# Two layers of cross-attention in fp32: scores in two rounded products instead of three, with the halves of the queries brought together by DMA

## The reference

```
q = x @ Wq;  k = ctx @ Wk;  v = ctx @ Wv          # fp32
s = softmax(q_h @ k_h.T / sqrt(16))               # per head, 256 x 77
x = x + concat_h(s @ v_h) @ Wo + bias
```

## Time and profile before

| | |
|---|---|
| median of 3 runs | 932.49 us (929.38 to 933.43) |
| span of the profiled execution | 926.1 us; its own time is not given beside it |
| TensorE matmul busy | 903.4 us (98%) |
| TensorE weight load busy | 681.3 us (74%) |
| VectorE busy | 685.7 us (74%) |
| ScalarE busy | 544.6 us (59%) |
| GpSimd busy | 402.8 us (43%) |
| granted TensorE clock, mean | 0.997 |
| DMA | 112.41 MB, 80526 packets, queue of SP busy 44.4% of 16 engines |

### The profile page before, as it was taken

How to read it: one execution, slowest core, us unless ns; L and a number is a source line. 1 busy time by engine, 2 the same in 40 slices (tenths; PEclk the granted TensorE clock), 3 DMA queues, 4 the chain that set the end, 5 groups by cost and what they waited for, 6 DMA issues and landing times.

```text
span 926.1 us, 28090 instructions
## 1 busy us (share of the span) xinstructions
PE 903.4 (98%) x11518; PEld 681.3 (74%) x11518; DVE 685.7 (74%) x1221; ACT 544.6 (59%) x549; POOL 402.8 (43%) x229
## 2 busy tenths in 40 slices
PE   8899999999999999999999999999999999999897
PEld 5777778777787777777777777777778777777665
DVE  3775787868778686787868688786786868678557
ACT  4456565656556556666556656556665656656553
POOL 3424263633436263366624446364344625433224
PEclk9999999999999999999999999999999999999999
DMA  6313534445444544545555444544534544443342
GB/s 203 102 32 80 138 93 132 135 124 148 98 119 119 164 131 110 149 115 140 141 148 140 102 118 113 137 132 123 134 95 118 139 131 134 102 130 78 86 134 94
DMA packets 80526, 112.41 MB, mean 121 GB/s; under 512 B 21200, under 2 KB 37878, under 8 KB 80400
## 3 DMA queue, kind: packets, MB, share of 16 engines
q1 hardware_dynamic: 80208, 110.35, 44.4%
q10 hardware_dynamic: 192, 0.26, 0.2%
HBM read 60.24 MB, written 22.24 MB: 89 GB/s over the span
## 4 chain that ended last, share of the span: by engine, by line
PE 82%; DVE 6%; DMA 4%; SPq 3%; issue 2%; ACT 1%; POOL 1%; DVEq 0%; ACTq 0%; POOLq 0%
PE pR L307 27%; PE pR L444 14%; PE pA L391 10%; PE pR L378 8%; PE pR L287 4%; PE pR L329 4%; PE pR L257 4%; DMA X<-in_xT 2%; PE pA L397 2%; PE pR L261 2%; DVE OS L1090 2%; SPq L1434 1%; PE pA L307 1%; DVE QL L995 1%; PE pR L244 1%
## 5 line engine op out<-in xcount | busy, mean ns | idle before, releaser
L763 ACT ACTIVATE P<-pA 77x2048 f32<-77x2048 f32 x160 | 300.4, 1878 | 197.2 <-PE pA L397 196.9
L1034 DVE TENSOR_REDUCE Mx<-pR 128x4 f32<-128x308 f32 (+1 forms) x480 | 259.2, 575 | 31.8 <-PE pR L378 26.6
L1293 POOL TENSOR_TENSOR On<-On,OS 128x1024 f32<-128x1024 f32 (+1 forms) x58 | 105.8, 1845 | 257.8 <-DMA OS<-rd 257.8
L307 PE MATMUL pR<-OS,Wo 128*128 128x512 f32 x638 | 168.1, 402 | 2.9 <-DVE OS L1090 2.1
L444 PE MATMUL pR<-P,VA 77*17 77x256 f32 x2480 | 157.4, 385 | 0.8 <-ACT P L763 0.5
L378 PEld LDWEIGHTS pR<-KH,QH 32*128 32x128 f32 x1280 | 96.3, 183 | 70.8 <-issue 46.6
L391 PE MATMUL pA<-QH,KH 32*77 32x256 f32 x1280 | 145.0, 291 | 0.1
L1258 POOL TENSOR_TENSOR XS<-X,XS 128x1024 fp32r<-128x1024 f32 x31 | 74.0, 2387 | 152.1 <-ACT XS L649 152.1
L378 PE MATMUL pR<-KH,QH 32*128 32x154 f32 x1280 | 131.5, 283 | 7.8 <-DVE X L1101 2.2
L307 PEld LDWEIGHTS pR<-OS,Wo 128*128 128x128 f32 x638 | 113.8, 188 | 33.2 <-issue 6.3
L391 PE MATMUL pA<-QL,KH 32*77 32x256 f32 x1280 | 134.9, 275 | 0.0
(11 more groups left out here) (161 smaller groups left out, 1289.6 us busy)
## 6 DMA issues: line engine op xcount, KB each, us to landing
On<-Oraw SPq DMA_DIRECT2D x244, 64.0 KB, 2.7
OS<-rd SPq DMA_DIRECT2D x58, 256.0 KB
C<-in_cT SPq DMA_DIRECT2D x16, 616.0 KB, 7.9
X<-in_xT SPq DMA_DIRECT2D x16, 512.0 KB
y<-X SPq DMA_DIRECT2D x16, 512.0 KB, 4.0
X<-y SPq DMA_DIRECT2D x16, 512.0 KB
out<-X SPq DMA_DIRECT2D x15, 512.0 KB, 4.0
X<-in_xT SPq DMA_DIRECT2D x16, 256.0 KB
```

What stands on the lines that cost most here:

```text
L307: f = pe.matmul(p[:, :], W[:, k, c0:c0 + 128], S[:, s, :], start=(i == 0), stop=(i == len(pairs) - 1))
L763: act.activation(P[0:L, i % PR, :, :], pA[0:L, :, :], ACT.Exp, scale=float(D) ** -0.5).then_inc(p_done, 1)
L1034: dve.tensor_reduce(Mx[:, :, :].rearrange("p t (j i) -> p j t i", j=4)[:, j:j + banks, :, i:i + 2], pR[:, bank:bank + banks, 0:2 * LK].rea ...
L1293: pool.tensor_tensor(On[rows, blocks, :], On[rows, blocks, :], recips(u, part).bitcast(F32), ALU.mult).then_inc(o_mul, 1)
```

## The change

The channels of queries and keys are reordered on the host so that the two heads of a 32-row block lie on its even (p = 0) and odd (p = 1) rows. The zeros of a head's keys are then on the other head's rows, and these rows get used: in `KL` the rows of the other head are filled by DMA with the high half of the keys (`keys`), and in the query tile of head p the rows of the other head with its low half (`queries_a` into `QH`, once the max products of that group have used it; `queries_b` into a new tile `TB`). One matmul with `KL` then gives low keys x high queries and high keys x low queries at once, and one with `KH` gives high x high. `QL` is single for channels 0 to 127 and for the last 64; for channels 128 to 255 it has two buffers (`QL1`). The subtraction for the low half of the last 64 channels' queries moves behind the first three reductions of the next pass, and waits for the query copies of the pass before. Keys have a padding column per head (`LP` = 78). The value tile has its ones so that a head's stationary operand is 32 columns, 16 channels and 16 times ones, alternating. That makes the results lie on alternate rows, so that `natural` takes 4 DMAs instead of 12. The reciprocals are written twice to DRAM, and one DMA of 16 pieces of 4 KB, each read by 8 rows, spreads them. `load_x` takes three DMAs instead of two. `V_last` has eight copies instead of two. SP's order is changed to hold the new DMAs.

```diff
-                for step in range(10):
+                for step in range(8):
...
-                    h = i // 3
+                    h = i // 2
...
-                    Q_ = (QH, QL, QH)[i % 3]
+                    q = QH[32 * j:32 * j + 32, u % 2, c0:c0 + SQ] if pp == 0 else TB[32 * j:32 * j + 32, c0:c0 + SQ]
                     if ms < 2:
-                        kt = (KH, KH, KL)[i % 3][32 * j:32 * j + 32, ms, u % 4, h, :]
+                        kt = (KH, KL)[i % 2][32 * j:32 * j + 32, ms, u // 2 % 2, pp, u % 2, h, 0:L]
...
                     if k % 2 == 0:
-                        pe.wait_ge(q_lo[ms], u + 1)
-                        pe.wait_ge(k_lo[ms], u // 2 + 1)
+                        pe.wait_ge(d_tb[ms], 32 * (u + 1))
+                        pe.wait_ge(d_k[ms // 2], 32 * (u // 2 + 1))
...
-                    if n is not None and step == 8:
+                    if n is not None and step == 6:
                         take_pair(second, 1)
...
-                        f = pe.matmul(bank[32 * j:32 * j + D + 1, b * SQ:b * SQ + SQ], VA[0:L, u % 2, b, h:C + H:H], src,
+                        f = pe.matmul(bank[32 * j:32 * j + 32, b * SQ:b * SQ + SQ], values_and_one(u, b, h), src,
...
+            pe.wait_ge(pads, 1)
```

VectorE (`Q_lo`, and its place in the loop):

```diff
                 dve.wait_ge(q_hi[m][u % 2], u // 2 + 1)
+                back = 2 if m == 1 else 1
+                if u >= back:
+                    dve.wait_ge(d_tb[m], 32 * (u - back + 1))
                 dve.tensor_tensor(lo, q, hi.bitcast(F32), ALU.subtract).then_inc(q_lo[m], 1)
...
                     elif u < NU - 2:
+                        Q_lo(u + 1, 2)
                         K_hi(w, 0)
                         split_o(z)
...
                     maxima(n, 4, 2)
-                    Q_lo(u + 2, 2)
                     Q_hi(u + 2, 1)
...
                 else:
                     maxima(n, 0, 1, 0, 2)
+                    Q_lo(u + 1, 2)
                     recip_last(v)
                     out(z, 0)
                     maxima(n, 1, 0)
...
                     maxima(n, 4, 2)
-                    if u < NU - 3:
-                        Q_lo(u + 2, 2)
                     Q_lo(u + 2, 0)
```

New functions of SP:

```diff
+            def keys(w, tail):
+                for m in ((0, 1), (2,))[tail]:
+                    sp.wait_ge(k_lo[m], w + 1)
+                for p in range(2):
+                    here, there = (EVEN, ODD) if p == 0 else (ODD, EVEN)
...
+                    sp.dma_start(lo[there].bitcast(F32), hi[here].bitcast(F32)).then_inc(d_k[tail], 16)
+            def queries_b(u, m):
+                cols = QCOLS[m]
+                sp.wait_ge(q_hi[m][u % 2], u // 2 + 1)
+                if u:
+                    sp.wait_ge(s_pe, NG * (u - 1) + (2, 4, 5)[m])
+                sp.dma_start(TB[ODD, cols].bitcast(F32), QH[ODD, u % 2, cols].bitcast(F32)).then_inc(d_ta[m], 16)
+                sp.wait_ge(q_lo[m], u + 1)
+                sp.dma_start(TB[EVEN, cols].bitcast(F32), low_queries(u, m)[ODD].bitcast(F32)).then_inc(d_tb[m], 16)
+            def queries_a(u, m):
+                cols = QCOLS[m]
+                sp.wait_ge(x_pe, 2 * (NG * u + (2, 4, 5)[m]))
+                sp.wait_ge(d_ta[m], 16 * (u + 1))
+                sp.dma_start(QH[ODD, u % 2, cols].bitcast(F32), low_queries(u, m)[EVEN].bitcast(F32)).then_inc(d_tb[m], 16)
```

The copies and the spread:

```diff
-                    for j in range(4):
-                        sp.dma_start(On[32 * j + D * r:32 * j + D * r + D, 0:2, :],
-                                     Oraw[32 * j:32 * j + D, r:r + 3:2, :]).then_inc(d_on[r], 16)
+                    sp.dma_start(On[64 * r:64 * r + 64, 0:2, :], Oraw[(EVEN, ODD)[r], 2 * r:2 * r + 2, :]).then_inc(d_on[r], 16)
...
+                for copy in range(2):
+                    if part == 0:
+                        sp.wait_ge(r_done, u + 1)
+                        heads = a["rd"][u, 0:32 * N].rearrange("(h q i c) -> q h i c", q=2, i=16, c=64)
+                        sp.dma_start(heads[copy], Zg[:, :]).then_inc(d_rw, 16)
...
-                for m in ((0, 1), (2,))[part]:
-                    src = a["rd"][u, 8 * m * N:min(8 * m + 8, H) * N].rearrange("(h o c) -> h o c", o=1, c=N)
...
+                    src = a["rd"][u, 0:32 * N].rearrange("(h o c) -> h o c", o=1, c=2 * N)
+                    sp.dma_start(recips(u, part).rearrange("p m n -> p (m n)").bitcast(F32),
+                                 src.broadcast_to([16, D // 2, 2 * N])).then_inc(d_rb, 16)
```

SP's order within a pass (even, then odd):

```diff
                     values(u + 1)
                     sums(v, 1)
                     for r in range(3):
                         natural(v, r)
+                    queries_b(n, 0)
                     put_recips(v, 0)
                     put_recips(v, 1)
+                    keys(w, 0)
+                    queries_a(n, 0)
                     spread(v, 0)
                     spread(v, 1)
                     store(z)
                     load_c(u // 2 + 2)
-                    sums(u, 0)
+                    queries_b(n, 1)
                     load_x(u + 3)
+                    queries_a(n, 1)
+                    queries_b(n, 2)
+                    keys(w, 1)
+                    queries_a(n, 2)
                 else:
                     sums(v, 2)
+                    sums(v, 0)
                     sums(v, 1)
...
                     natural(v, 1)
                     natural(v, 0)
+                    queries_b(n, 0)
                     natural(v, 2)
                     put_recips(v, 0)
                     put_recips(v, 1)
+                    queries_a(n, 0)
                     values(u + 1)
+                    queries_b(n, 1)
                     spread(v, 0)
                     spread(v, 1)
+                    queries_a(n, 1)
                     store(z)
                     sums(u, 0)
+                    queries_b(n, 2)
+                    queries_a(n, 2)
```

260 lines of the change are left out of this document (157 added, 103 removed).

## The result

The changed kernel takes 939.81 us (median of five runs, 936.71 to 940.67), against 929.38 us for the kernel before in the same session; the ratio is 1.0086, with a 95% interval of 1.0056 to 1.0116. It is slower, and just outside my range. The profiled execution took 940.67 us for a span of 938.9 us, 12.8 more than the span of before. The two profiles are not a typical pair: this one is the slowest of its five executions, and that of the kernel before, if its time also lies 1.8 us above its span, equals the fastest of its five.

The account below looks back on a forecast made before the run. It took TensorE to bound the kernel, with bank waits taking back much of the saving: 14 x 0.73 - 15 x 0.05 - 2.3 + 0.6 = 7.8 us, so 932.5 - 8 = 924.5 us; range 906 to 939.

Parts of the forecast that it names:

- The ceiling: TensorE's score matmuls: two steps saved in each of 32 x 5 runs, at most 37.7 us.
- Groups 0, 3 and 4 keep theirs: Even passes' score runs: these groups keep their saved steps, 0.83 us together, less 0.1 for the low query subtraction.
- groups 2, 3 and 4 keep 0.18 + 0.236 + 0.236: Odd passes' score runs: these groups keep 0.65 us of the saved steps, group 0 gains 0.
- The moved subtraction: VectorE in odd passes: it waits for GpSimd's context subtraction, ends 0.29 behind it, and costs 0.70 us a pass.
- rival (a): Odd passes: the moved subtraction falls between GpSimd's operations and costs nothing on the path; 912 us, chance 0.22.
- 0.15 a pass: SP's queue at the end of even passes: added DMAs delay the copies of sums, 2.3 us in all.
- rival (d): End of even passes: the last query copy and the sums behind it come late; slower, up to 946, chance 0.13.
- Together +0.6: First and last passes: saved steps and subtractions leaving VectorE's chain, against twelve more small ACT copies, gain 0.6 us.
- The sum: Whole kernel: the terms give 7.8 us less, span from 926.1 to 918.3, time 924.5 us.
- The loads of 32 columns: TensorE's value matmuls: 7 ns more a load, 17 us if all laid bare, taken as 0.
- the 6.4 us that I kept between the span and the time: Around the profiled span: the median of three runs, 932.5, lay 6.4 above it, and this was kept.
- three signs of being wrong: Subtraction takes 0.42 in odd passes, TensorE waits for a DMA at its scores, or odd passes shorten over 0.5 us.

Follow-up runs that it names:

- experiment 12: Kernel before with only the last 64 channels' low query subtraction moved behind the first three reductions in odd passes, run again for its profile; ratio 1.0108.
- sixth run: Changed kernel with query and low key copies between partitions made only in the first two passes; ratio to the kernel before 1.0311.
- experiment 1: Kernel before with the third score product left out, 8 steps in place of 10, nothing moved; ratio 0.9919, 922.90 us.
- tenth order: Second kernel with SyncE's DMAs reordered: copies that wait stand behind those that don't, last pass's sums ahead of its queries; ratio to the kernel before 0.9984.
- second kernel: Changed kernel with the odd passes' low query subtraction moved behind the copy of the second projection result; ratio to the kernel before 1.0039.
- 16: Tenth order with the last value products of only the first two groups issued together; ratio to the kernel before 0.9940, 927.78 us.
- 3: Changed kernel with last value products of groups 0 and 1 together, 2 and 3 together, heads ordered 0, 2, 1, 3; ratio to the kernel before 1.0202.
- 11: Tenth order with the last value products of groups issued in pairs, over four column blocks; ratio to the kernel before 0.9980.

## Why the prediction was wrong

**The ceiling** stands: the saved steps are there, TensorE issues 2560 score products for 3840. What failed is the step behind it.

**"Groups 0, 3 and 4 keep theirs", "groups 2, 3 and 4 keep 0.18 + 0.236 + 0.236" is the step that failed first.** I looked for a late bank only where the run follows a projection or a sum that was on my rows, and took the step count for the take point elsewhere. In nine of the ten places a run takes its second pair only behind a copy, sum or emptying of what TensorE made ahead of it, 0.84 us or more from its start, where the steps alone would allow 0.71. (That it waits for that bank is read from the times and the order of banks; no run moved a bank.) Groups 3 and 4 keep 0.04 to 0.05 of 0.236, in even and in odd passes; group 1 of even passes and group 2 of odd ones, for which I had 0.12 and 0.18, keep nothing. Only group 0 of even passes keeps 0.18. Measured without the rest, an even pass gains 0.48 for my 0.73 and an odd one 0.17 for my 0.65, and passes 0 to 29 gain 8.8 us where I had 20.5 (14 x 0.73 + 0.5 + 15 x 0.65): 11.7 us gone, enough by itself to turn a gain of 0.8% into nothing.

**The moved subtraction**: the mechanism was right in place, length and end (0.28 behind GpSimd's end, forecast 0.29; pass 21: 1.55 us). The full 0.90 by which the emptying comes later is lost in a pass, where I took 0.70 with some slack in between; but only 13 of the 15 odd passes lose it. In all it costs 9.8 us in the profile of experiment 12, for my 15 x 0.70 = 10.5, which is luck in part. The Trainium skill, SBUF — State Buffer, section Who interferes with whom, has a VectorE instruction with two SBUF inputs contend with a GpSimd instruction that reads SBUF, for an exclusive lock. The trace agrees, in that the subtraction ends only behind GpSimd's operation, but 0.28 behind it and not the full 0.42 that the prediction drew from that page. The sixth run shows how wide it reaches. My rival (a) is thereby refuted.

**The queue.** "0.15 a pass" is not how it comes. Most odd passes lose nothing to it; two, 5 and 23, lose 1 to 3 us. In pass 5 it was a wait of SyncE for a landing, then one of VectorE for the late query copy and for the sums, then the lower clock. That is my rival (d), a query copy at the end of even passes that comes late, only in single passes and not in all 15. Without the copies (6) these exceptions are gone. What is left in passes 0 to 29 once experiments 1 and 12 are taken out, -8.8 and +9.8, is 5.7 us of the changed kernel's +6.7, for my 2.3. It holds these exceptions, and whatever the wider loads, the copies of keys and the new forms add; this was not taken apart. The tenth order has a ratio 0.55% below the second kernel's, some 5 us, but their profiles differ by only 1.2 us in passes 0 to 29, so this price is open too.

**"Together +0.6", the edges, is the second step that failed.** I counted the passes' saved steps there and twelve small copies, and did not look at what the diff shows: that the new block order gives the last value products of groups 0 to 3 two column blocks instead of four. That is 7 us of TensorE. Pairing the first two groups (16 against 10) takes 3.8 us off the stretch from pass 31 on, 39.8 for 43.6, one slow call's length; two slow calls, 3.5 us, are left against 36.5 in the kernel before. That the queries stand ahead of the sums in the last pass (8 us later against the pass's start) I had not looked at either, but it costs little: with the sums first (10) the stretch takes 0.7 us less, at the same granted clock of 0.96. Pairing all four groups (3, 11) opened a gap and lowered the clock. Measured: -1.7 in pass 30 and +7.8 behind it, where I had +0.6 in favour; 1.7 of the 7.8 are a fall of the clock that other executions of the kernel before's own order of passes have too.

**The sum.** From -7.8 to +12.7 (926.15 to 938.88) are 20.5 us: 11.7 for the banks, 6.1 for the edges and 3.4 for the queue and what else is in passes 0 to 29, less 0.7 for the subtraction. The loads of 32 columns were mis-sized in length (142 ns in the mean for 113; I had 7 ns more), but like the new form of the reductions (576 ns in the mean, 575 before) they hardly reach the time: experiment 1 has neither, and the tenth kernel, which has both, comes within 0.65% of it. And the 6.4 us that I kept between the span and the time were not that: an execution takes 1.8 us more than its span, the rest is the spread of executions.

None of my three signs of being wrong came up: the subtraction took 1.55 us, the profile shows no wait of TensorE for a DMA at its scores, and odd passes got longer. They all asked after the parts that I had thought about. The length of the runs of groups 3 and 4, on which 4 x 0.236 of the 1.38 us per pair of passes rested, was not among them.

## What to carry to other kernels

A step taken off the bottleneck is worth only what the next bank, buffer or semaphore in its own stream lets through: measure, for each kind of run, the time from its start to its second take, and whose end that is. Put an instruction of VectorE with two SBUF inputs where GpSimd is idle, and when a transfer gets faster or slower ask what GpSimd's operation behind it will then lie beside. Ahead of a queue's time-critical copies nothing may stand that waits for a landing. An end without cover, the last pass, is to be read by itself, and there by TensorE's busy time as well as by the chain of waits, which names the wait that ended last and not its price. And price a gap in TensorE's work together with the clock behind it.

## What I had not expected of the hardware

- A spread of 512 KB of reciprocals from 16 pieces is used 4.86 us after its issue, from 8 pieces 6.99 us after; and the slowest query copy into `QH` lands 8.3 us after its issue with the latter, 5.2 with the former.
- TensorE's column blocks work beside each other over several products: 32 take some 1.9 us in three orders that change blocks within four, 2.81 with eight in turn on two blocks, 3.61 on two blocks alone.
- Holding work back to issue it better can cost more than it saves: after 1.22 us busy in 4.5, the granted clock stood at 0.50 for 19 us. Shorter gaps do it too: after 0.19 us busy in 2 it stood at 0.50 for the next 2.
- Eleven DMAs a pass fewer made the kernel 2% slower.
